# VectorE's routing work moved ahead of a normalisation, and TensorE's turn of the mask moved behind one more product

## The reference, cut to what matters

```
x = x + ga * (attention output)                     # residual, gated per batch
h = layernorm(x) * (1 + cb) + sb
router_logits = h @ router_w + router_b             # 8 experts
routing_weights = softmax(router_logits)
top_k_weights, top_k_indices = top_k(routing_weights, 2)
top_k_weights = top_k_weights / sum(top_k_weights)
routing_mask = zeros.at[..., top_k_indices].set(top_k_weights)     # (token, 8)
h1 = gelu(einsum('btd,nde->btne', h, W1) + b1)      # 8 experts, 128 hidden each
out = einsum('btne,nef->btnf', h1, W2) + b2
x = x + gb * sum(out * routing_mask[..., None], axis=-2)
```

## Time and profile before

| | us |
|---|---|
| median of 3 runs (lowest, highest) | 5026.35 (5023.26, 5029.09) |
| the profiled execution | 5039.53 |
| its span | 5038.0 |
| granted TensorE clock over the span | 0.947 |
| PE busy, share of the span | 4661.5 (93%) |
| DVE busy | 4141.8 (82%) |
| ACT busy | 3503.2 (70%) |
| POOL busy | 1374.1 (27%) |
| this mixture: first projection to last product | 2899 to 3539 |

### The profile page before, as it was taken

How to read it: one execution, slowest core, us unless ns; L and a number is a source line. 1 busy time by engine, 2 the same in 40 slices (tenths; PEclk the granted TensorE clock), 3 DMA queues, 4 the chain that set the end, 5 groups by cost and what they waited for, 6 DMA issues and landing times. The chain is left out here.

```text
span 5038.0 us, 108786 instructions
## 1 busy us (share of the span) xinstructions
PE 4661.5 (93%) x35325; PEld 2561.6 (51%) x35325; DVE 4141.8 (82%) x6451; ACT 3503.2 (70%) x6777; POOL 1374.1 (27%) x1290
## 2 busy tenths in 40 slices
PE   8689999999999999999999879999699999965998
PEld 6533333333333333333333357777466666655887
DVE  6689999999999999999999856666577877775554
ACT  3358888888888888888888723333477877744554
POOL 1321111111111111111111133333234344445776
PEclk9879999999999999999999989999799999956999
DMA  8941222222222122212222123232100000044552
GB/s 264 297 113 39 44 52 44 45 43 46 55 44 44 35 53 53 44 39 44 52 44 48 31 87 106 88 116 89 39 29 20 29 20 22 27 160 151 167 165 95
DMA packets 247818, 375.78 MB, mean 75 GB/s; under 512 B 61567, under 2 KB 172690, under 8 KB 238732
## 3 DMA queue, kind: packets, MB, share of 16 engines
q1 hardware_dynamic: 231440, 312.27, 24.7%
q0 software_dynamic: 15904, 57.38, 3.1%
HBM read 241.16 MB, written 136.46 MB: 75 GB/s over the span
## 5 line engine op out<-in xcount | busy, mean ns | idle before, releaser
L833 DVE TENSOR_REDUCE at_mxp<-at_ps_m 128x2 f32<-128x1024 f32 x2092 | 2526.2, 1222 | 78.5 <-PE at_ps_m L886 52.5
L764 ACT ACTIVATE at_prob<-at_ps_s 128x512 f32<-128x512 f32 x4100 | 2227.4, 596 | 331.7 <-PE at_ps_s L876 300.5
L896 PE MATMUL at_ps_o<-at_prob,at_vs 128*32 128x256 f32 x16384 | 1313.9, 393 | 14.0 <-ACT at_osum L770 14.0
L876 PE MATMUL at_ps_s<-at_qs,at_ks 51*128 51x512 f32 x4100 | 1038.0, 501 | 4.7 <-DMA at_qs<-t_largest 4.2
L886 PE MATMUL at_ps_m<-at_ks,at_qs 49*128 49x512 f32 x4184 | 858.4, 406 | 49.7 <-DMA at_ks<-t_alibi 36.5
L876 PEld LDWEIGHTS at_ps_s<-at_qs,at_ks 51*128 51x128 f32 x4100 | 385.1, 184 | 854.2 <-ACT at_prob L764 849.1
L896 PEld LDWEIGHTS at_ps_o<-at_prob,at_vs 128*32 128x32 f32 x16384 | 324.4, 108 | 776.8 <-issue 389.8
L556 POOL TENSOR_TENSOR at_total<-at_total,at_minus 128x16 f32<-128x16 f32 x65 | 190.4, 2929 | 1132.6 <-DMA at_total<-at_osum 1132.6
L886 PEld LDWEIGHTS at_ps_m<-at_ks,at_qs 49*128 49x128 f32 x4184 | 404.6, 190 | 71.6 <-DMA at_ks<-t_alibi 36.9
L1297 ACT ACTIVATE mi_act<-mi_ps_h,mi_b 128x512 f32<-128x512 f32 x131 | 89.9, 686 | 351.4 <-PE mi_ps_h L1385 350.9
L68 DVE TENSOR_TENSOR ex_hidc<-ex_hid,ex_hidc 128x512 fp32r<-128x512 f32 x128 | 154.8, 1219 | 161.6 <-ACT ex_hid L2643 161.6
(11 more groups left out here) (322 smaller groups left out, 6403.6 us busy)
## 6 DMA issues: line engine op xcount, KB each, us to landing
mi_spread<-t_masks SPq DMA_DIRECT2D x68, 512.0 KB, 4.9
t_parts<-pr_parts SPq DMA_DIRECT2D x64, 512.0 KB, 6.8
at_ks<-t_parts SPq DMA_DIRECT2D x102, 256.0 KB
t_buf<-at_blank POOLq DMA_DIRECT2D x64, 384.5 KB, 3.3
at_qs<-t_parts SPq DMA_DIRECT2D x96, 256.0 KB
at_vs<-t_v SPq DMA_DIRECT2D x17, 1024.0 KB
ex_rest<-t_buf SPq DMA_DIRECT2D x16, 1026.0 KB, 5.3
t_v<-pr_vaug SPq DMA_DIRECT2D x64, 256.0 KB, 5.8
```

What stands on the lines that cost most here:

```text
L764: nc.scalar.activation(prob[0 if up is None else (t + 1) % 2][:, j, :], ps_s[bank][:, :], ACT.Exp).then_inc(s_read, 1)
L833: nc.vector.tensor_reduce(out[:, s4, k + i, 2 * pair:2 * pair + 2], ps_m[i][:, :, :], AX.X, ALU.max).then_inc(mx_read, 1)
L876: nc.tensor.matmul(ps_s[bank][:, :], ks[s][a:a + QROWS, j // 2, t1 * P:(t1 + 1) * P], qs[s][a:a + QROWS, j // 2, c * T:(c + 1) * T], start ...
L896: last = nc.tensor.matmul(ps_o[32 * j:32 * j + 32, q0:q1], vs[s][:, t, 32 * j:32 * j + 32], prob[t % 2][:, j, q0:q1], start=(t == 0 and ha ...
```

## The change

On DVE `best_two` gets one comparison more: `iota` (0 to 7 along the free dimension) against both choices of all four groups at once, one tensor_tensor over 64 elements, with `ixf` laid out choice first. In `routing` the eight small tensor_scalar operations (compare and multiply, 8 elements each) give way to one tensor_tensor multiplication over 64 elements. `first_norm` moves from in front of `weigh(i, 5)` to behind `routing`, in front of `weigh(i, 7)`. On PE `up(i+1, 1)` comes in front of `down(i, 6)` and `turn_masks` behind it. On ACT `hidden(i+1, 1)` comes in front of `turned_masks`. What comes before the loop keeps its order.

```
-        ixf, gap, e2 = sb("ixf", [P, SUB, 2]), sb("gap", [P, SUB]), sb("e2", [P, SUB])
+        ixf, gap, e2 = sb("ixf", [P, 2, SUB]), sb("gap", [P, SUB]), sb("e2", [P, SUB])
...
                     dve.drain()
-                    nc.vector.tensor_copy(ixf[:, :, :], ix[:, :, 0:2])
+                    nc.vector.tensor_copy(ixf[:, :, :], ix[:, :, 0:2].rearrange("p s k -> p k s"))
+                    dve.drain()
+                    nc.vector.tensor_tensor(pick[:, :, :, :].rearrange("p k s e -> p (k s) e"), iota[:, :].unsqueeze(1).to_broadcast([P, 2 * SUB, E0]),
+                                            ixf[:, :, :].rearrange("p k s -> p (k s)").unsqueeze(2).to_broadcast([P, 2 * SUB, E0]), ALU.is_equal)
...
                 def routing(h):
 
                     dve.drain()
-                    for k in range(2):
-                        for s in range(SUB):
-                            nc.vector.tensor_scalar(pick[:, k, s, :], iota[:, :], ixf[:, s, k:k + 1], wt[:, k, s:s + 1], ALU.is_equal, ALU.mult)
+                    flat = pick[:, :, :, :].rearrange("p k s e -> p (k s) e")
+                    nc.vector.tensor_tensor(flat, flat, wt[:, :, :].rearrange("p k s -> p (k s)").unsqueeze(2).to_broadcast([P, 2 * SUB, E0]), ALU.mult)
                     dve.drain()
...
                         weigh(i, 4)
                         upper_rows(i + 1, h1)
-                        first_norm(i + 2, h)
                         weigh(i, 5)
                         best_two(i + 1)
                         weigh(i, 6)
                         two_weights(i + 1)
                         routing(h1)
+                        first_norm(i + 2, h)
                         weigh(i, 7)
...
                         hidden(i + 1, 0)
+                        hidden(i + 1, 1)
                         turned_masks(i + 1, (c + 1) % 2)
-                        hidden(i + 1, 1)
                         hidden(i + 1, 2)
...
                         down(i, 5, b)
+                        up(i + 1, h1, 1)
+                        down(i, 6, b)
                         turn_masks(i + 1, h1)
-                        down(i, 6, b)
-                        up(i + 1, h1, 1)
                         down(i, 7, b)
                         up(i + 1, h1, 2)
```

## The result

The changed kernel takes 4958.84 us in the median of four runs (4951.97 to 4962.7); the kernel before, in the same comparison, 5027.72 (5023.26 to 5035.61). The ratio is 0.9857, 95% interval 0.9841 to 0.9873. It is faster, as forecast, but by about 69 us where 57.7 had been worked out, and the median lies 1.2 us under the low end of the wider range (4960). The profiled execution took 4962.7, with a span of 4961.1 and a granted clock of 0.951.

The account below looks back on a forecast made before the run. PE was taken as bound, idle only ahead of the mask's turn, where DVE and POOL shut each other out. 53.0 + 7.0 + 1.1 − 2.5 − 0.9 = 57.7 us less: 4969, range 4962 to 4978, wider 4960 to 4989.

Parts of the forecast that it names:

- The waits that go: PE's sixteen waits ahead of the mask's turn vanish: 47.4 us idle plus 16 × 0.35, 53.0 us.
- The clock: PE's slower clock behind five long waits ahead of the mask's turn recovers: 5 × 1.40, 7.0 us.
- The mask in time: DVE's mask would come at about 3194.9, PE reach its new place at 3198.99: 4.1 us early.
- rival B: In a batch's last chunk weigh 6 or 7 comes late behind POOL's gated weights: 14 us, 4982; chance 0.07.
- The moved norm: First norm behind the routing: weigh 7 ends two us before PE wants it, 0.6 in a batch's last chunk.
- rival C: POOL's base pair gets ahead of weigh 7 in each chunk, price 4.9 us: 5033 to 5050; chance 0.03.
- What is late next: Mask's DRAM round trip keeps 1.1 us of cover before the normed rows; two early turns late, cost 0.9 us.
- rival A: Spread mask becomes the limit, its DRAM round trip landing later: PE waits 18 us, 4987; chance 0.12.
- Both ends: Before the loop, fewer picks gain 1.1 us; at the end, the later store of `x2` costs 2.5.
- Sum: All terms together 57.7 us less, taken from the median 5026.35: 4968.7, told as 4969.

Follow-up runs that it names:

- e8: Changed kernel plus a drain and eight small DVE memsets between first norm and weigh 7, so POOL starts first; 4976.33 us, ratio 0.9919.
- e7: Changed kernel with the turn of the mask still later, behind expert 7's product and the third hidden product; 5015.94 us, ratio 0.9989.
- e1: The kernel before, unchanged, run again; 5025.22 us, ratio 0.9996.
- e2: The changed kernel, unchanged, run again; 4962.20 us, ratio 0.9873 to the kernel before.
- e6: Kernel before with only the single comparison and multiplication replacing the eight picks, none of the three moves; 4997.88 us, ratio 0.9961.
- e3: Kernel before with DVE's changes alone, PE's and ACT's orders as before; 4948.33 us, ratio 0.9856.

## Why the prediction was right or wrong

**The waits that go.** Right, and mis-sized: I put 0.35 us of extra time on each of 16 waits. The undisturbed turn comes 1.72 after a product's start and not 1.54, so the extra is 0.17 and the term 50.1, not 53.0.

**The clock.** Right: the chunks behind a batch's last turn now run at 1.00 throughout, as said, and such a chunk took 36.8 before where others took 35.3, 1.5 for the 1.40 taken. Waits and clock together brought 53.2 us over the fifteen periods from turn to turn (553.9 before, 500.7 after). The 53.0 that the prediction names as the sum without this term is the waits' term alone; the whole sum without it is 50.7.

**The mask in time.** Right: the mask is early everywhere, and the new operations take 0.22 and 0.23 us against the 0.25 taken. In a batch's last chunk POOL did shut out weigh 6 (4.12), and so rival B's mechanism exists, with 3.2 us of cover left for weigh 6 and 1.8 for weigh 7.

**The moved norm and rival C.** Weigh 7 went first in every chunk. C's mechanism exists, but its price was wrong: one operation of POOL, about 1.9 us (2.57 less 0.68), instead of the pair's 4.9. In e8, which brings C about, the mixture was 5.4 longer, so C would not have made this kernel slower than before.

**What is late next and rival A.** The cover was 0.9 (1.1 said), and the one early turn that became late lengthened its chunk by 0.8 (34.13 for 33.33, with an idle time of 0.4 in it; 0.9 said). That one product more uses the cover up, e7 shows; I had the wrong consumer, since the projection and expert 0's product wait before the normed rows do.

**Both ends.** From the first projection to the first turn the gain was 0.6 us in this pair (34.6 to 34.1). Over all profiles it is 1.2, from 35.0 on average in the five with the old picks to 33.8 in the twelve with the new operations, so the 1.1 was right. The stretch from the last turn to the scan went only from 22.9 to 22.5: the end takes back what the later turn moved in front of it. The issue of the store came as said, 5.5 us after the turn (8.0 before), but from there to the scan's first statistics it took 17.1 us where it had taken 14.9. The prediction had put 0.5 on that, so this term is short by 1.7. Here are the rows of after, and then the scan's first row in the kernel before, whose store is in the earlier trace rows:

```profile
3480.91 0.62 SPq L1060 DMA_DIRECT2D t_x<-mi_x  x1
3497.97 1.41 DVE L1656 BATCH_NORM_STATS2 sc_st<-sc_xin 128x6 f32<-128x256 f32 x4 [4.82 <-DMA sc_xin<-t_x]
```

```profile
3554.06 1.41 DVE L1654 BATCH_NORM_STATS2 sc_st<-sc_xin 128x6 f32<-128x256 f32 x4 [4.51 <-DMA sc_xin<-t_x]
```

**Sum.** This is the step that failed. The mixture gave 52.7 for the 57.7 worked out. Of the 5 too much, 2.9 is the turn (16 × 0.18), 1.7 the end, and 0.5 the front of this pair. The sum then let the whole program move with the mixture alone ("from the median: 5026.35 − 57.7"). It put the phases outside the mixture at nothing, and gave them no width. Between the two profiled executions, 24 us lay outside the mixture: 9.2 in the scan, 9.2 in the second mixture, 2.3 in the readout, 3.4 before the mixture. Between e1 and e2, 7.3 did. In the medians it is 16 and 8. So the two errors have opposite signs, and that the median lies only 1.2 us outside the range is partly luck. A readout 2.3 shorter belongs to the change. In the scan 8.2 of the 9.2 are the same matmuls taking longer (PE busy 836.5 and 828.3), by a clock that falls behind a wait or does not. Two executions of one kernel differ as much: the kernel before had a second mixture of 414.1 and of 404.2. Why what is left of the medians of the kernels with the new routing lies on the lower side each time stays open. The prediction itself had said that a measurement tells about 10 us from no change, and then put the low end of its wider range only 9 us below the forecast; some 10 us more on that side would have been due.

**The parts.** The place of the first norm is worth 50 of the 53 us, the operations on picks alone 16, PE's and ACT's part alone 37; they remove the same wait, so they do not add. The third part, on top of DVE's, costs 5.

## What to carry to other kernels

When two engines shut each other out, first look for the operation that releases the other engine's long work, and move that one behind the critical chain; shortening or postponing the chain itself is second. When one reordering already clears a wait, each further one has to be run alone, since its cost (here a later round trip) stays while its gain is gone. And a forecast for a whole program needs a width for the phases that the change doesn't touch: profiled executions of the same kernel tell how much (here 13.5 us in the scan of three, 9.9 in the second mixture of two).

## What the runs showed of the hardware

- A DVE operation with both inputs in SBUF that meets a long POOL operation ends with it, whatever its size: 0.22 us became 2.21, 0.65 became 4.12. In the kernel before, between 2950 and 3475 us, all 41 such operations that began with over 1 us of POOL's operation left were held. The others that began so were not, 149 of them: maximum and index search (0.07 to 0.17 us) and the additions with one input in PSUM (0.17 and 0.68 us, with up to 2.3 us of POOL's operation left).
- Between POOL operations with a drain between them a waiting one slips in (e8, 2.57 us); between the bias rows and the weights, and between the weights and the base (the gap in e6, 4.61), which have none, it did not.
- A wait of 0.49 us in e7, 7 us behind another of 0.89, was followed by a product at nearly half speed (3.67 for 1.89); one of 0.45 in e8 by none, and one of 2.40 in e3's scan by none. In one execution of after, two of four waits of 2.2 to 2.4 us at the same line were followed by the lower clock and two were not.
- Of one kernel, the kernel before, 72 runs (e1's and those beside the experiments) ranged from 4999 to 5047 us, and their granted clock over the span from 0.953 to 0.944, the fastest run having the highest.
- 28 one-element memsets in idle time of DVE lengthened a later phase of unchanged code by 3 us, twice (188.2 and 188.3 to 191.4 and 191.2), and moved DVE's idle times of 1.5 to 2.9 us without a releaser to other instructions.
